# Self-attention: the low part of the transposed weights ahead of the scores' maximum in VectorE's step

## The reference

```
h = _rms(x, ln_w)
q, k, v = h @ wq, h @ wk, h @ wv          # 32, 8 and 8 heads of 64
q, k = _rope(q, k)
scores = einsum('bqhd,bkhd->bhqk', q, k) / sqrt(64)
scores = where(causal, scores, -1e30)
attn = softmax(scores, -1)
o = einsum('bhqk,bkhd->bqhd', attn, v)
x = x + o @ wo
```

## Time and profile before

| what | us |
|---|---|
| median of 3 runs | 2742.99 |
| lowest and highest run | 2740.89, 2746.09 |
| the profiled execution, its own time | 2737.78 |
| its span | 2736.0 |
| TensorE busy in the span | 2392.1 |
| VectorE busy | 1704.6 |
| ScalarE busy | 1487.6 |
| GpSimd busy | 1097.8 |

### The profile page before, as it was taken

One profiled execution on the slowest core, in us unless ns is written; L12 is line 12 of the kernel. 1 busy time (PEld: TensorE's weight loads), 2 busy tenths in 40 slices (PEclk: granted clock), 3 DMA queues, 4 the chain that ended last, 5 costly groups with the idle time before them and its releaser, 6 DMA issues.

```text
span 2736.0 us, 46215 instructions
## 1 busy us (share of the span) xinstructions
PE 2392.1 (87%) x14819; PEld 1988.6 (73%) x14828; DVE 1704.6 (62%) x3850; ACT 1487.6 (54%) x3094; POOL 1097.8 (40%) x1556
## 2 busy tenths in 40 slices
PE   5999999999996598889888856699999579989988
PEld 3787878878875588888888735699999467777754
DVE  2555555555555456666666566465556578888876
ACT  3644444444444566666666436344444277777765
POOL 0223222222230344444444327577777274444410
PEclk9999999999998699999999978799999799999999
DMA  3310000000013100000000056576766564224000
GB/s 131 113 30 8 19 12 8 19 12 19 8 59 126 43 20 20 19 19 0 19 19 19 1 168 208 185 194 188 190 188 172 119 185 101 59 58 100 9 5 31
DMA packets 147525, 198.38 MB, mean 73 GB/s; under 512 B 21924, under 2 KB 85796, under 8 KB 147044
## 3 DMA queue, kind: packets, MB, share of 16 engines
q1 hardware_dynamic: 131672, 160.70, 19.9%
q0 software_dynamic: 10992, 25.96, 4.4%
q10 hardware_dynamic: 4768, 10.62, 1.2%
HBM read 151.09 MB, written 46.15 MB: 72 GB/s over the span
## 4 chain that ended last, share of the span: by engine, by line
PE 69%; DVE 11%; ACT 7%; issue 6%; DMA 4%; POOL 2%; DVEq 0%; SPq 0%; ACTq 0%; POOLq 0%
PE pair L2271 8%; PE pair L655 7%; PE pair L1199 5%; PE pair L1249 5%; PE pair L683 4%; PE pair L2762 4%; PE pair L616 4%; PE pair L2289 3%; PE pair L641 3%; PE pair L1271 3%; PE pair L2745 3%; PE pair L1233 2%; PE pair L2777 2%; PE pair L612 2%; PE pair L622 2%
## 5 line engine op out<-in xcount | busy, mean ns | idle before, releaser
L531 ACT ACTIVATE x_p<-x_p,x_least 128x1024 f32<-128x1024 f32 x128 | 147.2, 1150 | 279.2 <-DVE x_least L482 279.2
L587 POOL TENSOR_TENSOR x_carry<-x_rtotal 128x1 f32<-128x1 f32 x128 | 24.9, 195 | 575.2 <-DVE x_rtotal L459 575.2
L466 DVE TENSOR_TENSOR x_pT<-pair,x_pT 128x512 fp32r<-128x512 f32 x256 | 164.3, 683 | 125.2 <-ACT x_pT L552 125.2
L2271 PE MATMUL pair<-m_h,e_w 128*128 128x320 f32 x1536 | 229.6, 310 | 1.1 <-DVE m_h L2186 1.1
L2271 PEld LDWEIGHTS pair<-m_h,e_w 128*128 128x128 f32 x1536 | 228.1, 189 | 2.7 <-issue 1.5
L655 PE MATMUL pair<-x_pT,x_v 128*128 128x256 f32 x1536 | 214.5, 298 | 13.9 <-DVE x_pT L466 13.9
L655 PEld LDWEIGHTS pair<-x_pT,x_v 128*128 128x128 f32 x1536 | 198.6, 198 | 30.7 <-issue 22.5
L1111 ACT ACTIVATE s_p<-s_p,s_least 128x128 f32<-128x128 f32 (+3 forms) x256 | 143.6, 561 | 123.3 <-DVE s_least L1021 123.3
L683 PE MATMUL pair<-x_kT,x_qT 128*128 128x512 f32 x768 | 208.1, 406 | 0.0
L1249 PE MATMUL pair<-s_pT,s_v 128*128 128x256 f32 (+1 forms) x1152 | 158.6, 284 | 47.8 <-DVE s_pT L998 47.8
L1249 PEld LDWEIGHTS pair<-s_pT,s_v 128*128 128x128 f32 x1152 | 153.1, 196 | 60.1 <-issue 30.7
(11 more groups left out here) (351 smaller groups left out, 6097.0 us busy)
## 6 DMA issues: line engine op xcount, KB each, us to landing
e_raw<-in_L_ffn_w SPq DMA_DIRECT2D x48, 1024.0 KB, 5.7
z_kS<-z_k SPq DMA_DIRECT2D x24, 512.0 KB, 9.6
hslot<-in_L_ffn_w ACTq DMA_DIRECT2D x16, 512.0 KB, 3.6
hT_x<-in_L_ffn_w SPq DMA_DIRECT2D x16, 512.0 KB, 5.3
z_v<-z_vst SPq DMA_DIRECT2D x16, 512.0 KB, 3.0
z_vS<-z_v SPq DMA_DIRECT2D x8, 960.0 KB, 9.7
z_qS<-z_q SPq DMA_DIRECT2D x24, 256.0 KB, 4.3
s_wraw<-in_L_ffn_wq SPq DMA_DIRECT2D x9, 512.0 KB, 4.4
```

The costliest lines, as they stand in the source:

```text
L466: dve.tensor_tensor(pT[1][:, keys, q * P:(q + 1) * P], TR[j][:, :].rearrange("p (k n) -> p k n", n=P), pT[0][:, keys, q * P:(q + 1) * P].b ...
L531: act.activation(p[n][:, :], p[n][:, :], ACT.Exp, scale=-1.0, bias=least[:, n:n + 1], accum_out=total[:, n:n + 1]).then_inc(s_ex, 1)
L2271: mm = pe.matmul(GU[m % 2][:, j * BANK:j * BANK + CAP], w[x0][:, c, m * P:(m + 1) * P], XS[s][x1][:, c, :], start=(n == 0 and c == 0), sto ...
```

## The change

In each step of VectorE, the call of `low` stands ahead of the wait for the scores, the reciprocal and the maximum, and no longer behind them. Its condition is the same. ScalarE's, TensorE's, GpSimd's and SyncE's orders are the same.

```diff
--- before.py
+++ after.py
@@ -1013,6 +1013,8 @@
                             low_outputs(PPB - 1, h - 1)
                         if own and n == PAIR_DONE + 1:
                             low_outputs(0, h)
+                        if n - LAG - 1 >= 0 and own or before and n <= LAG:
+                            low(n - LAG - 1)
                         if own:
                             dve.wait_ge(s_sc, NS * h + n + (2 if q == 0 else 1))
                             reciprocal(n - 2)
@@ -1023,8 +1025,6 @@
                                 least[:, n % RING:n % RING + 1]).then_inc(s_sm, 1)
                         elif n < 2:
                             reciprocal(n - 2)
-                        if n - LAG - 1 >= 0 and own or before and n <= LAG:
-                            low(n - LAG - 1)
                         for t in range(QT):
                             if before and n == OUT[t]:
                                 add_out(t)
```

## The result

The changed kernel takes 2800.84 us (median of 4 runs, 2797.38 to 2811.78), the kernel before 2743.51 us (now also of 4 runs, 2740.89 to 2746.09). The ratio is 1.0218, with a 95% interval of 1.0201 to 1.0235: slower by 57 us, where 56 were forecast. The profiled execution is the slowest of the four, 2811.78 us, and that of before lies 5.7 us under its median. Of the 74 us between the two, 66.5 lie in self-attention (from its first stacked copy to its last addition of an output) and 8 behind it.

What follows compares the result with a forecast made beforehand. TensorE sets self-attention's pace with some 11% gaps; the change closes a chain longer than the turn. Even turns 29.8, odd 18.6, edges 8, clock 0 sum to 56 us; 2743 + 56 = 2799 us, range 2766 to 2832.

Steps and rivals of the forecast that it cites:

- The order and the chain: Self-attention, VectorE and ScalarE: high part, low part, maximum, exponential become one closed chain, 2.02 us a step.
- the replay: Hand timing of an even and an odd self-attention turn, each instruction starting when its engine is free and its releaser ended.
- Where it decides: TensorE covers the chain in steps 0 to 4; steps 5 to 15 hold 20.5 us of its work against 29 us.
- The size of the full turns: Turns 1 to 14: 4.25 us per even and 2.65 us per odd turn, 29.8 and 18.6 us.
- The clock: TensorE's lower clock behind gaps before step 8's values: taken as 0, between -5 and +22 us.
- The edges: Turns 0 and 15: 4 us each, 8 together, between 0 and 8 each; the turn after the last 0.
- The signs: Profile after: ScalarE's minimum wait towards 200 us, VectorE's scores wait under a third, TensorE's waits up some 50 us, turns longer.
- The sign of being wrong: Forecast wrong if ScalarE's wait for the minimum falls or TensorE's gaps before line 1249 shrink in steps 8 to 15.
- (a): Rival: TensorE, 87% busy, absorbs the later maximum and the earlier low part about pays; 2743 us within 5; chance 0.05.
- (d): Rival: the order hardly matters, because VectorE comes late to both waits; same time; chance 0.02.
- (c): Rival: chain as forecast, and every full turn falls to the lower clock at 1.6 us; 2821 us; chance 0.10.
- (b): Rival: faster, since the low part never waits for scores, its place being step 7; 2731 us; chance 0.05.

Runs made afterwards that it cites:

- the dose on ScalarE: Four more unread 128x512 copies a turn on ScalarE, in both kernels: changed kernel 2847.60 us (2800.84 without them), kernel before 2743.90 us (2743.51 without).
- steps 5 to 15 alone: Against the kernel before, the low part first only in steps 5 to 15 of a turn: 2798.75 us, ratio 1.0206.
- the kernel with the filled gaps: Changed kernel with ten more scores matmuls in step 8 and eight in step 14 on TensorE, overwritten by the real ones: 2792.60 us, ratio 1.0193.
- the output weights moved: Kernel before with GpSimd's rounding and low part of the output weights in steps 1 and 2 of odd turns, not 3 and 4: 2739.46 us.

## Why the prediction was right, point by point

- **The order and the chain**: right. High part, low part, maximum, exponential follow each other with nothing beside them; the replay met five starts of the first three steps within 0.1 us, and the dose on ScalarE shows the chain closed after and open before.
- **Where it decides**: right for steps 5 to 15, all of the loss. "Steps 0 to 4 cost nothing" holds for the maximum, but not for what stands behind the reciprocal on GpSimd: alone they cost 23 us, by a collision that lengthens a gap a little and the lower clock that follows it. In the full change that isn't seen: its median lies 2 us above that of steps 5 to 15 alone, less than the runs can tell.
- **The size of the full turns**: 48.4 us forecast (4.25 and 2.65 us in an even and an odd turn). Without falls of the clock (from the kernel with the filled gaps) the pair costs 42.8 - 38.75 = 4.05 and 42.0 - 39.2 = 2.8, by seven 48. The inner terms erred against each other: the addition of the rotation took 0.9 us, not 2.0 (by the row 0.76 less at the first copy), and the rest of the turn lost 0.6 more.
- **The clock**: taken as 0, between -5 and +22, on the ground that its cost would lie under a late chain. Mis-sized, and the gaps it was hung on were half wrong: 2.24 us in even turns, but 1.64 in odd ones, where 2.3 had been foreseen; many falls came behind another gap, that of 1.7 us ahead of the stacked queries. First copies of turn 0 and 14 are 550.3 us apart before, 606.8 after: 56.5 more. Of these 48 are the chain; the falls came to 606.8 - 7 x 84.8 = 13 us after and 4.6 before, so +9. Filling the gaps brought back 13 us in turns 1 to 14 of the traces, 8.2 between the medians.
- **The edges**: 8 us forecast. Turn 0 lost 3.5 us and the stretch from the last first copy to the stage's last addition 6.5 (60.1 to 66.5), in this profiled execution.
- These terms sum to 67 us, for an execution that was 11 us above the median. The kernel with steps 5 to 15 alone, profiled near its own median, has 603.6 us in turns 1 to 14 and 59.9 in the last stretch: there the clock costs some 6 us more than before and the late edge nothing. So part of the exact hit (2799 against 2800.8) is luck: the clock and the edges vary from run to run by as much as they were missed.
- **The signs**: VectorE's wait for scores fell and the distances between turns grew, as said. The sign of being wrong, that TensorE's gaps before line 1249 shrink in steps 8 to 15, was met in part: in step 8 of odd turns the gap shrank by 0.6 us while that of even turns grew by 1.0, and the waits as a whole rose from 47.8 to 55.3 us. The sign was badly put, since one gap can shrink in a turn that gets longer. ScalarE's wait for the minimum rose further than I said (264, not 200), since nearly every step is in the chain, covered or not. TensorE's own waits for line 998 and the first stacked copies (9.1 us before) rose by some 25 us, not 50, while its busy time in the stage rose from 569.8 to 607.1 us for the same matmuls, at a lower mean clock. As the falls cost only some 9 us, I conclude that most of that lies where TensorE would have waited anyway.
- **Rivals**: (a) and (d) fell with the whole; (c), the clock, was a part, at 9 us instead of 22; (b) was right about step 7 and wrong about the rest, as the run with step 7 alone shows.
- Rule and row: the Trainium skill, page "Perfetto Trace Analysis", section "Identifying the Most-Contended Engine", takes the engine of highest occupancy as the bottleneck. That is TensorE, at 87%, and one would infer that a dose on ScalarE, at 53%, is free. Here it was all but free before and cost 47 us after; the measurement decides. The Trainium skill, page "SBUF — State Buffer", section "Who interferes with whom", says that an instruction of VectorE with two SBUF inputs contends with one of GpSimd that reads SBUF, and that the order of issue decides which of the two is held up. The traces agree: 2.36 us for the addition where GpSimd was first, 0.89 us, and 2.41 instead of 1.84 for GpSimd, where VectorE was.

## What to carry to other kernels

Before two operations of an in-order engine are swapped, draw the ring that the new order closes with the engine it talks to, add up its latencies from start to start, and compare the sum with the bounding engine's work in that stretch, not over the whole kernel. An operation that may wait belongs ahead of one that starts another engine only in the steps where the trace shows its input already there; here step 7 was such a step, and the low part first in it alone made a loss of 57 us into a gain of 13. Follow also what is queued behind a delayed release on a third engine, since it may come to run beside work that it slows.

## What the runs showed that was not expected

- The lower clock level (1.2 GHz, half of the full 2.4) came irregularly behind the same gap, that ahead of the values of step 8: behind 2.2 us in three of seven turns of the kernel before, behind 1.77 us in three of seven with the output weights moved, behind 2.50 us in six of seven, behind 1.5 us in none of seven with the low part first in step 7. In the kernel with the reciprocal first it came directly behind the 2.2 us gap of even turns in none of seven, so the length of a gap alone doesn't decide.
- An instruction with two tensor inputs from SBUF on VectorE took up to 2.36 us instead of 0.81 beside a GpSimd subtraction that had started 0.16 us earlier. Where VectorE started first, GpSimd paid instead: its subtraction of 128x512 grew from 1.28 us in the mean to 1.55 in the changed kernel.
- A change that only reorders waits altered TensorE's busy time in the stage by 37 us, for the same number of matmuls.
